# Local attention: probabilities turned in blocks by VectorE, gathered values in two buffers, output product in three parts, another order on VectorE and ScalarE

## The reference, cut to what matters

```python
def local_attention(q, k, v):              # after l2norm and rotary tables
    bq = q.reshape(b, h, nw, w, d)         # w = 32
    bk2, bv2 = (look(bk), look(bv))        # each window with the one before it: 64 keys
    sim = jnp.einsum('bhwie,bhwje->bhwij', bq, bk2) * QK_SCALE
    sim = jnp.where(mask, -jnp.finfo(sim.dtype).max, sim)
    attn = jax.nn.softmax(sim, -1)
    out = jnp.einsum('bhwij,bhwje->bhwie', attn, bv2)
...
x = out.transpose(0, 2, 1, 3).reshape(b, n, INNER) @ Wo
...
hg = layernorm(x) @ W1 + b1
a, gate = jnp.split(hg, 2, -1)
x = a * gelu(gate) @ W2 + b2
```

## Time and profile before

| | us |
|---|---|
| runs | 4609.84, 4618.05, 4621.47; median 4618.05 |
| profiled execution | 4616.27 |
| its span, first to last instruction | 4614.5 |
| run 0 of the local attention, about | 576 to 2340 |
| run 1 of the local attention, about | 2818 to 4610 |

### The profile page before, as it was taken

One profiled execution on the slowest core, in us unless ns is written; L12 is line 12 of the kernel. 1 busy time (PEld: TensorE's weight loads), 2 busy tenths in 40 slices (PEclk: granted clock), 3 DMA queues, 4 the chain that ended last, 5 costly groups with the idle time before them and its releaser, 6 DMA issues. The chain is left out here.

```text
span 4614.5 us, 133631 instructions
## 1 busy us (share of the span) xinstructions
PE 4320.6 (94%) x57968; PEld 2899.1 (63%) x57968; DVE 2891.1 (63%) x3838; ACT 2273.4 (49%) x2592; POOL 2746.8 (60%) x3511
## 2 busy tenths in 40 slices
PE   8999889999999999999967876999999999999997
PEld 3333357676766776767736663676767667677674
DVE  1575167767767677777634335677776776767773
ACT  2454245555555555555521112555555565555553
POOL 0000077777777777777604114877777777777772
PEclk9899989999999999999976557999999999999998
DMA  0000000000000000000000001000000000000000
GB/s 17 1 1 1 23 34 11 11 16 11 2 17 11 16 11 2 7 2 2 2 7 4 4 4 56 11 11 2 16 11 16 12 2 16 11 7 2 2 2 10
DMA packets 14134, 46.53 MB, mean 10 GB/s; under 512 B 3808, under 2 KB 6240, under 8 KB 11744
## 3 DMA queue, kind: packets, MB, share of 16 engines
q1 hardware_dynamic: 13536, 37.83, 2.4%
HBM read 36.78 MB, written 1.05 MB: 8 GB/s over the span
## 5 line engine op out<-in xcount | busy, mean ns | idle before, releaser
L718 POOL TENSOR_TENSOR w_qk<-w_turned 128x1024 f32<-128x1024 f32 x384 | 904.4, 2355 | 119.0 <-DVE w_turned L601 89.6
L596 DVE TENSOR_TENSOR w_turned<-w_ps_qk,w_rot_l 128x1024 f32<-128x1024 f32 x384 | 469.9, 1224 | 719.7 <-ACT w_squares L498 700.0
L255 PE MATMUL w_ps_qk<-w_w_qk,ZT 128*128 128x512 f32 x1536 | 751.7, 613 | 37.1 <-DVE w_turned L601 18.2
L305 PE MATMUL w_ps_y<-w_px,w_w_vo 128*128 128x128 f32 x6144 | 752.5, 276 | 7.0 <-ACT w_px L502 6.7
L305 PEld LDWEIGHTS w_ps_y<-w_px,w_w_vo 128*128 128x128 f32 x6144 | 722.5, 193 | 31.8 <-issue 21.0
L747 POOL TENSOR_TENSOR w_qk<-w_qk,w_inv_norm 128x1024 f32<-128x1024 f32 x384 | 722.8, 1904 | 0.0
L498 ACT ACTIVATE w_squares<-w_ps_qk 128x1024 f32<-128x1024 f32 x384 | 391.3, 1019 | 436.5 <-PE w_ps_qk L255 436.1
L601 DVE TENSOR_TENSOR w_turned<-w_ps_qk,w_rot_l 128x1024 f32<-128x1024 f32 x384 | 466.5, 1215 | 0.0
L605 DVE TENSOR_REDUCE w_sumsq<-w_squares 128x16 f32<-128x1024 f32 x384 | 455.4, 1186 | 0.0
L502 ACT ACTIVATE w_px<-w_ps_t 128x1024 f32<-128x1024 f32 x192 | 196.5, 1024 | 509.7 <-PE w_ps_t L297 509.7
L255 PEld LDWEIGHTS w_ps_qk<-w_w_qk,ZT 128*128 128x128 f32 x1536 | 266.7, 194 | 266.7 <-issue 240.9
(11 more groups left out here) (254 smaller groups left out, 7349.5 us busy)
## 6 DMA issues: line engine op xcount, KB each, us to landing
w_w_qk<-in_w_qk SPq DMA_DIRECT2D x12, 1024.0 KB, 4.9
w_w_vT<-in_w_vT SPq DMA_DIRECT2D x12, 512.0 KB, 3.7
w_w_o<-in_w_o SPq DMA_DIRECT2D x12, 512.0 KB, 4.7
w_w<-in_w SPq DMA_DIRECT2D x12, 384.0 KB, 3.1
w_w<-in_w SPq DMA_DIRECT2D x12, 192.0 KB, 3.1
XT<-in_x SPq DMA_DIRECT2D x1, 1024.0 KB, 4.8
w_rot<-in_rot SPq DMA_DIRECT2D x2, 512.0 KB, 5.9
out<-XT SPq DMA_DIRECT2D x1, 1024.0 KB, 3.9
```

The costliest lines, as they stand in the source:

```text
L255: last = nc.tensor.matmul(ps_qk[:, c, :], Z[:, T.col:T.col + P], w_qk[:, T.parity, cols], start=True, stop=True)
L305: last = nc.tensor.matmul(ps_y[:, D.t * P:(D.t + 1) * P].rearrange("p (a v q) -> p a v q", a=2, q=WIN), w_vo[:, D.parity, h, p, :], px[:, ...
L596: nc.vector.tensor_tensor(turned[:, which, 0, :].rearrange("p (h d) -> p h d", d=DH), flat(ps_qk[:]).rearrange("p (h d) -> p h d", d=DH), ...
L718: nc.gpsimd.tensor_tensor(qk[:, T.odd, which, :], turned[:, which, 0, :], turned[:, which, 1, :], ALU.add).then_inc(pool_add, 1)
```

## The change

What it does, in the order of the engines:

- The tokens are transposed once per shift: `x_tok` holds, for each tile, the 128 tokens and the 128 tokens that lie one window earlier. That is two transposes a tile instead of four, and the two extra ones of each sequence (`edge`) are gone. ScalarE's copy is 256 columns instead of 512.
- The probabilities are no longer transposed by TensorE. VectorE transposes them in blocks of 32 by 32 (`nc.vector.transpose`) from `probs` into `pT`, which has another layout; `turn_probs` and ScalarE's copy L558 are gone.
- `gather` is one burst of eight products: each uses 32 rows of the array (one window's 32 keys), 512 columns (16 heads by 32 queries), window w on row group w into bank w; the two key halves are added up in PSUM. `ps_t` and `ps_s` become two halves of one tile `ps_w`, and the gather writes all of it. ScalarE copies banks 2 and 3 first, then 0 and 1. `px` has two buffers.
- The scores of B now wait for the first of these copies (C), and the next turning of q for the second.
- `output` comes in three parts: 5 pairs, 1 or 2 pairs (2 in gate and up steps), and the last 2 or 1 between the gather and the scores.
- On TensorE `place_1` comes before the second `project`; the broadcast L400 moves up to `place_2` unless weights are merged in the step; `place_4` is gone.
- On ScalarE the exponential moves from the end of the step to the next step's start, behind the first square; the second square moves behind the copies of `place_1`; a one-element exponential (`warm`) is put at the end of an up step.
- On VectorE the row sums and the reciprocal come before the first `rotate`, the block transpose after it; maximum and subtraction come after the second sum of squares and the root preparation; the normalising L664, the third `hidden` and the addition of `ps_y` come last.
- On GpSimd the scaling of `probs` comes before the first `add`.

```diff
+        x_tok = sb("x_tok", [P, TILES, 2, DIM])
+        pT = sb("pT", [P, 2, HEADS, WIN])
+        px = sb("px", [P, 2, WINS, HEADS, WIN])
+        ps_w = ps("ps_w", [P, 4, 512])
+        ps_t, ps_s = ps_w[:, 0:2, :], ps_w[:, 2:4, :]
...
+            def tokens(B):
+                for half in range(2):
+                    at = B.col - WIN * (1 - half)
+                    last = nc.tensor.transpose(ps_f[:, half * P:(half + 1) * P], Z[:, at:at + P], ident[:])
+                last.then_inc(pe_xt, 1)
...
-            def turn_probs(C):
-                for p in range(PAIRS):
-                    last = nc.tensor.transpose(ps_t[:, p // 4, (p % 4) * P:(p % 4 + 1) * P],
-                                               probs[:, 2 * p:2 * p + 2, :].rearrange("p h k -> p (h k)"), ident[:])
-                last.then_inc(pe_pt, 1)
...
+            def gather(C):
+                for half in range(2):
+                    for w in range(WINS):
+                        rows = slice(w * WIN, (w + 1) * WIN)
+                        last = nc.tensor.matmul(ps_w[:, w, :], x_tok[rows, C.t, half, :],
+                                                pT[rows, half].rearrange("p h q -> p (h q)"),
+                                                start=half == 0, stop=half == 1)
                 last.then_inc(pe_px, 1)
...
     # TensorE, step
-                if D:
-                    if C:
-                        pe.wait_ge(dve_sub, C.n + 1)
-                    gather(D, 1, ps_s)
                 if B:
                     pe.wait_ge(pool_qk, B.n * 2 + 1)
                     if D:
-                        pe.wait_ge(act_px, D.n * 2 + 1)
+                        pe.wait_ge(act_px, D.n * 2 + 2)
                     turn(B, 0, pe_tq)
...
-                    output(D, range(PAIRS // 2))
+                    output(D, range(5))
...
+                last_pairs = 7 if s.gate or s.up else 6
                 if D:
-                    output(D, range(PAIRS // 2, PAIRS)).then_inc(pe_y, 1)
+                    output(D, range(5, last_pairs))
+                place_1(s)
                 if T:
                     pe.wait_ge(dve_turn, T.n * 2 + 1)
                     project(T, 1, pe_k)
-                place_1(s)
                 if C:
                     if B:
                         pe.wait_ge(act_tk, B.n + 1)
-                    pe.wait_ge(pool_p, C.n + 1)
-                    turn_probs(C)
+                    pe.wait_ge(dve_sub, C.n + 1)
+                    pe.wait_ge(dve_pt, C.n + 1)
+                    pe.wait_ge(act_xt, C.n + 1)
+                    gather(C)
                 place_2(s)
+                if D:
+                    output(D, range(last_pairs, PAIRS)).then_inc(pe_y, 1)
                 if B:
                     pe.wait_ge(act_tk, B.n + 1)
-                    if D:
-                        pe.wait_ge(act_px, D.n * 2 + 2)
-                    elif C:
-                        pe.wait_ge(dve_sub, C.n + 1)
+                    if C:
+                        pe.wait_ge(act_px, C.n * 2 + 1)
                     scores(B)
                 place_3(s)
...
     # VectorE, step: behind rotate(T, 0) and the down addition
+                if C:
+                    dve.wait_ge(pool_p, C.n + 1)
+                    if D:
+                        dve.wait_ge(pe_px, D.n + 1)
+                    nc.vector.transpose(pT[:].rearrange("p a h q -> p h a q"),
+                                        probs[:].rearrange("p h (a k) -> p h a k", a=2)).then_inc(dve_pt, 1)
```

228 lines of the change are left out of this document (99 added, 129 removed).

## The result

The changed kernel takes 4566.48 us (median of 4 runs, 4562.01 to 4570.35) against 4619.76 for the kernel before in runs beside it: a ratio of 0.9885, with a 95% interval of 0.9868 to 0.9901. It is 53 us faster. The prediction was 4449 with a range of 4365 to 4530: the sign is right, the size is not, and the time lies 36 us above the range. The profiled execution took 4568.15 us, its span is 4566.4.

A forecast was written before the change was run, and what follows sets the result against it. TensorE's stream was taken as the bound until hand-overs replace it. A layer gains 20.7 - 2.3 - 2.8 - 1.0 - 0.5 = 14.1 us, twelve layers 169, giving a median of 4449 us, range 4365 to 4530.

The forecast's parts named there:

- what TensorE is spared: TensorE's stream: transposes and gather save 1.24 us a step, 20.7 us a layer with the edge transposes.
- the doubtful term: The gather on TensorE: eight products on 32 rows take 2.04 us instead of 2.14, sparing 0.10 us a step.
- Case (c): Gather: row groups overlap only two at a time, 3.44 us instead of 2.04, so slower at 4718 us; chance 0.08.
- The block transpose: VectorE, after rotate: 1.25 us, hidden from the gather; twice as long would cost 0.7 us in three steps of four.
- the term for VectorE's late step: Up step's VectorE tail, sum of squares and roots at 1.96 us, running into down steps: 2.8 us a layer lost.
- rotate (second project): Norm steps: TensorE's second project waits 1.25 us in the plain one, 0.35 in three others; 2.3 us a layer.
- `hidden` (down product): Down steps: TensorE's down product, due at 2.8 us, waits 0.3 us for VectorE's hidden.
- `xn` (token transposes): After the two norm steps without a merge, token transposes wait 0.5 us for VectorE's normalising; 1.0 us a layer.
- `Z` (centring): Down steps: the centring product before the second project waits 0.4 us for VectorE's down addition.
- A second term: Filling and draining of the pipeline, left at nothing: fewer operations against a longer wait for the exponential.
- (b): Hand-over chain bounds every step: 0.6 us longer than laid out, all but down steps lose, 4528 us; chance 0.12.
- (a): TensorE stays the only bound: the 6.6 us of waits a layer are gone, 4370 us; chance 0.17.

## Why the prediction was off

**What bounds the kernel** was read rightly: TensorE's stream, and behind it a chain over VectorE. So was what TensorE is spared: 236 us by its busy time, 248 in the sum.

**The gather**, called the doubtful term: 1.93 us against 2.04. Case (c) is out; all four row groups overlap. The estimate from the Trainium skill ("TensorE: Matmul & The Clock Gate", section "Measured speedup vs the span model"), 2.24 us, was further off than the trace's own row: eight products of 0.86 us in 1.93 are a speedup of 3.6, not 3.07.

**The block transpose**: 1.237 us on average, forecast 1.25 from an operation with another source. It is hidden, as said: the gather waits for it 5 us in the whole run, and a second one costs 80 us where the lay-out gave 100.

**The step that failed** is the term for VectorE's late step, in the paragraph on the down steps: "hidden, sum of squares and roots (3569.29, where VectorE falls idle, minus 3566.19 and 1.14: 1.96)". It took the duration of the root operations from a place where GpSimd's addition had already ended (3566.8 against a root operation at 3568.58, at 0.18 us) and moved it to a place right behind the second rotate, the very operation that starts that addition. There the first one takes 1.44 us on average. The rows of before that show the old place (start, us):

```profile
3564.46 2.35 POOL L718 TENSOR_TENSOR w_qk<-w_turned 128x1024 f32<-128x1024 f32 x1
3568.58 0.18 DVE L688 TENSOR_SCALAR w_halved<-w_sumsq 128x36 f32<-128x36 f32 x1
```

Sum of squares and roots were 1.96 us in the sum. After the change, from the start of the sum of squares to that of the maximum, they take 2.90 us in the up step of the stretch above, and 3460.26 - 3455.72 = 4.54 in its gate step:

```profile
3473.79 1.21 DVE L582 TENSOR_REDUCE w_sumsq<-w_squares 128x16 f32<-128x1024 f32 x1
3475.03 1.22 DVE L651 TENSOR_SCALAR w_halved<-w_sumsq 128x36 f32<-128x36 f32 x1
...
3476.69 1.22 DVE L661 TENSOR_REDUCE w_neg_max<-w_ps_w 128x16 f32<-128x1024 f32 x1
```

The 0.94 us that the term is short in this up step are what the down product waits more behind it: 1.26 us for `hidden` instead of 0.3. The prediction asked of moved work only what it waits for and who waits for it, and not what runs beside it in the new place. On average 1.2 us more in each of 192 steps stand ahead of maximum and subtraction.

The Trainium skill ("SBUF — State Buffer", section "Who interferes with whom") has the rule: `tensor_scalar` on VectorE can take the port pair that it shares with GpSimd, and whoever issues second blocks fully, while `tensor_reduce` never contends. The rows here agree: 220 against 1435 ns for the one; and for the reduction 1.19 us for the sum of squares, of which 382 of 384 run beside a long operation of GpSimd in the changed kernel. The prediction did not weigh it, and should have, since it speaks against this change.

**What it did to the waits**, in us of the whole run; the forecast is what the sum had for twelve layers:

| TensorE waits for | before | forecast, added | after | added |
|---|---|---|---|---|
| rotate (second project) | 18.2 | 28 | 53.8 | 36 |
| `hidden` (down product) | 3.4 | 14 | 51.2 | 48 |
| `xn` (token transposes) | 1.7 | 12 | 38.1 | 36 |
| `Z` (centring) | 3.2 | 19 | 15.6 | 12 |
| `qT` (turning of k) | 5.5 | 0 | 29.8 | 24 |
| nothing shown, inside the scores | 8.4 | 0 | 34.1 | 26 |
| scaled or turned probabilities | 20.2 | 0 | 5.1 | -15 |

The two that the prediction gave to rotate and centring came out near it. Of the 50 waits for rotate 18 stand in the first steps of the two runs (29.0 us, where before 18.2 us stood). The other 32 are in norm steps, 24.8 us: about 1.3 in the plain ones (forecast 1.25), 0.24 in those that merge weights (0.35). The centring product waits 0.25 us in most down steps (0.4). Of the wait for `qT` 18.5 us stand in the first steps too. `hidden`, `xn` and `qT` stand behind the subtraction on VectorE or behind the exponential on ScalarE: 108 us added instead of 26. The exponential itself waits for the subtraction 81 times, 68 us in all. With the root operations unheld these fall, and the time with them, by 67 us in the kernel that moves the maximum and by 83 with the short addition. That is 57 to 71% of the 117 us between forecast and result.

**A second term** was put at nothing, filling and draining of the pipeline. From TensorE's first product of a run to the mask product of its eighth tile, and from the last mask product to the end, the two runs together gain 4 us; the 16 steps that this stands for would gain 14 by the sum's rate. In the steps between, 49 us are gained where the sum has 155.

**What is left** without the hold, 35 to 50 us, is accounted for only in part. The profiled execution of the changed kernel lies 121 us above the 4447 of the sum: 12 because TensorE's busy time fell by 236 and not by 248, and 109 because its idle time rose by 188 and not by 79. The rows of the table hold 167 of the 188; the other 21 are spread over small rows. With the maximum ahead of the roots, the first five rows of the table add 84 us, near the sum's 79. What stands beside them there are pauses in the middle of the 128 small products of the scores, for which no semaphore or engine is named: 41.7 us, 32 times, as against 34.1 in the changed kernel and 8.4 before. In 23 of the 25 of them that last 0.8 us or more in the changed kernel the DMA engines move nothing, so that transfers are not their cause. And the clock: the sum had none of it. At the end of the same four steps TensorE pauses and the granted clock drops (windows of after, columns as above):

```profile
3511.00:3513.40 2.40, 0.67 (x27) 0.49 (x12) 2.33 (x5) 0.00 (x0) 1.53 (x5) 1.00 0.70 275
3514.30:3517.60 3.30, 3.30 (x6) 1.30 (x6) 1.11 (x2) 0.00 (x0) 1.55 (x7) 0.54 0.03 7
```

In the second window the clock is at 0.54 of full speed, close to the lower of its two levels (1.2 of 2.4 GHz), after 2.4 us in which TensorE was busy for 0.67. The project there takes 3.25 us instead of 1.72 from start to start, 1.5 us on top of the wait:

```profile
3513.44 1.03 PE L404 MATMUL w_ps_f<-ident,w_rstd 128*128 128x128 f32 x6 [1.77 <-issue]
3514.26 3.41 PE L252 MATMUL w_ps_qk<-w_w_qk,ZT 128*128 128x512 f32 x4
3517.51 1.04 PE L258 MATMUL w_ps_w<-ident,w_qk 128*128 128x128 f32 x8
```

Between the eighth and the last tile of each run, one group of TensorE's timeline took over 1.5 times the median of its kind before (1.6 us beyond it), and six after (9.0 us). These are part of TensorE's busy time, and so of the 12 us above. No experiment here takes the pauses or the clock away, so their share was read, not shown.

**The rivals.** (b), the chain a bound in every step at 4528, is nearest in time, and it is not what happened in every step: the gate step above runs in 16.01 us without a wait. But the sign that the prediction named for being wrong, a wait in gate and up steps, is there in up steps: 1.22 us for `qT` at 3464.94, behind the gate step in which GpSimd folds the scales, and eleven such waits in the whole run, 10 us. (b)'s remark that VectorE may reach the subtraction late, so that the exponential waits for it, was the right place, with no cause named; that its 4528 lies nearer than the forecast is in part luck. (a) left the waits out, and they came.
